# Second graph pass: the x strip on its own semaphore, the second mean square from the variance, the last two strips' keys stacked by SP

## What is computed

```python
def _L0_gnn_ref(x, adj, W):
    A_hat = adj + jnp.eye(adj.shape[0])
    d_inv_sqrt = jnp.sum(A_hat, axis=1) ** (-0.5)
    A_norm = d_inv_sqrt[:, None] * A_hat * d_inv_sqrt[None, :]
    return jax.nn.relu(A_norm @ (x @ W.T))

x = x + _L0_gnn_ref(_layernorm(x), adj, W)      # x1 in the kernel
z = _layernorm(x)                               # (x - mean) / sqrt(var + 1e-5)
h = z * rsqrt(mean(z * z) + 1e-6) * ln1_w       # the attention's input norm
q, k, v = h @ wq.T, h @ wk.T, h @ wv.T          # q and k are then rotated by cos, sin
...                                             # attention, experts
```

## Time and profile before

| | us |
|---|---|
| median of three runs | 3701.52 (3696.71 to 3705.01) |
| the profiled execution | 3697.04 |
| its span on the core | 3695.3 |

### The profile page before, as it was taken

The page is one execution under the profiler, slowest core; times in us unless marked ns, Lnnn a source line. Parts: engine busy times, 40 slices in busy tenths (PEclk is TensorE's granted clock), DMA queues, the critical chain, the costliest instruction groups (busy, mean ns, idle before and its releaser), DMA issues. The chain is left out here.

```text
span 3695.3 us, 56800 instructions
## 1 busy us (share of the span) xinstructions
PE 3115.2 (84%) x22369; PEld 1368.1 (37%) x22369; DVE 2580.5 (70%) x2752; ACT 1424.4 (39%) x2843; POOL 1690.7 (46%) x1094
## 2 busy tenths in 40 slices
PE   2578898999677884999999999999999999839990
PEld 1334443444333342343333333333333333315650
DVE  8888786773343443778878987877987898326773
ACT  0000000000000001565666666666666666735660
POOL 0000000002111111566788688877689778744653
PEclk9778999999888996999999999999999999969995
DMA  9898777676555762542221000000000000012226
GB/s 378 351 398 354 318 318 289 251 305 226 213 221 212 278 252 74 201 147 79 92 91 61 13 15 22 13 7 7 7 18 17 10 4 16 11 53 66 75 64 230
DMA packets 170238, 531.94 MB, mean 144 GB/s; under 512 B 20721, under 2 KB 66554, under 8 KB 125062
## 3 DMA queue, kind: packets, MB, share of 16 engines
q1 hardware_dynamic: 123752, 473.35, 33.3%
q10 hardware_dynamic: 33024, 31.47, 2.6%
q0 software_dynamic: 13200, 23.50, 2.0%
HBM read 434.70 MB, written 92.15 MB: 143 GB/s over the span
## 5 line engine op out<-in xcount | busy, mean ns | idle before, releaser
L1202 DVE TENSOR_REDUCE unit_max<-ps_max 128x2 f32<-128x1024 f32 (+2 forms) x1088 | 1226.1, 1171 | 310.5 <-PE ps_max L1431 265.6
L978 POOL TENSOR_TENSOR chunk_sum<-chunk_sum,probs 128x1024 f32<-128x1024 f32 x480 | 1132.2, 2359 | 307.9 <-ACT probs L1072 297.8
L1072 ACT ACTIVATE probs<-ps_ring 128x512 f32<-128x512 f32 x2112 | 1089.8, 595 | 437.1 <-PE ps_ring L1450 403.1
L537 PE MATMUL ps_gather<-ring,keep_attended 128*128 128x512 f32 x1688 | 803.1, 633 | 138.3 <-DMA ring<-in_adj 115.1
L1450 PE MATMUL ps_ring<-q_stack,keep_shared 97*128 97x512 f16 x2112 | 673.4, 385 | 27.8 <-ACT probs L1072 22.1
L1465 PE MATMUL ps_acc<-probs,keep_shared 128*32 128x256 f32 (+1 forms) x8448 | 565.6, 386 | 0.0
L537 PEld LDWEIGHTS ps_gather<-ring,keep_attended 128*128 128x128 f32 x1688 | 338.2, 205 | 548.4 <-issue 548.4
L352 DVE TENSOR_TENSOR work<-work,ring 128x2048 f32<-128x2048 f32 x195 | 446.7, 2291 | 38.8 <-DMA ring<-in_adj 35.0
L322 POOL DMA_DIRECT2D scratch_lower<-lower x13 | 7.3, 559 | 803.7 <-ACT lower L460 803.7
L1431 PE MATMUL ps_max<-k_heads,q_heads 32*128 32x512 f16 (+3 forms) x2176 | 277.0, 379 | 74.9 <-DVE unit_max L1202 48.2
L1474 PE MATMUL ps_acc<-probs,keep_ones_heads 128*32 128x256 f32 (+1 forms) x4224 | 326.9, 378 | 0.0
(11 more groups left out here) (239 smaller groups left out, 2742.3 us busy)
## 6 DMA issues: line engine op xcount, KB each, us to landing
ring<-in_adj SPq DMA_DIRECT2D x302, 1024.0 KB, 14.1
keep_shared<-in_adj SPq DMA_DIRECT2D x45, 1024.0 KB, 10.2
scratch_slots<-empty_rows SPq DMA_DIRECT2D x16, 2080.0 KB, 14.1
scratch_parts<-empty_part SPq DMA_DIRECT2D x8, 2048.0 KB, 13.3
moe_parts<-scratch_parts SPq DMA_DIRECT2D x64, 256.0 KB, 4.5
moe_x_rows<-scratch_slots SPq DMA_DIRECT2D x39, 260.0 KB, 2.7
x_in<-in_x SPq DMA_DIRECT2D x16, 256.0 KB, 13.2
x_in<-in_x ACTq DMA_DIRECT2D x16, 256.0 KB, 4.1
```

What stands on the lines that cost most here:

```text
L537: last = nc.tensor.matmul(bank[:], support[:, s * SUB + c, :], tile_of[g, is_again][:, c * BT:(c + 1) * BT], start=(first and c == 0), sto ...
L978: steps.then(nc.gpsimd.tensor_tensor(totals, totals, weights, ALU.add))
L1072: nc.scalar.activation(probs[:, q % SLOTS, i, kv, :, lo:], halves(bank)[:, :, lo:], ACT.Exp, scale=SCALE).then_inc(ring_read, 1)
L1202: nc.vector.tensor_reduce(unit_max[:, half % 2, heads, s % 2, unit], ps_max[:, base:base + HEADS, at:at + width], AX_X, ALU.max).then_inc( ...
```

## The change

- x has its own semaphore. Its load moves from behind `rotate(n)` to behind the first square root of `normalize(n)`, ahead of the stores of x1 and z. L411 waits for x alone. cos and sin stay where they were, under a new semaphore `tables_loaded`, for which `rotate` waits.
- The sum of squares of the centred rows is kept in `centered_sum`, and the mean square of z is taken from it as sum / C / std / std: three instructions on 128 x 4 values in the place of two on 128 x 512 and one on 128 x 4.
- The keys of the last two strips (n = 14 and 15) are stacked by SP, behind its last ring loads, under `last_stacked`. POOL issues those of the first fourteen and ends after its subtractions. SP waits for all stackings at the stage's end.

```diff
+        STACKED_BY_POOL = NB - 2
+        def stack_keys(queue, n, stacked):
+            cols = slice(finished[n] * BT, (finished[n] + 1) * BT)
+            for kv in range(NKV):
+                row = kv * NREP * HD
+                for part, src in ((0, k_hi), (1, k_lo), (2, k_hi)):
+                    queue.dma_start(keep["k_stack"][part * HD:(part + 1) * HD, kv, cols],
+                                    src[row:row + HD, :]).then_inc(stacked, 16)
...
                 for s in again[t]:
                     load_group((t, s), True)
+            for n in range(STACKED_BY_POOL, NB):
+                sp.wait_ge(stack_ready, 1)
+                sp.wait_ge(split_ready, 2 * n + 2)
+                stack_keys(sp, n, last_stacked)
+            sp.wait_ge(keys_stacked, 96 * STACKED_BY_POOL)
+            sp.wait_ge(last_stacked, 96 * (NB - STACKED_BY_POOL))
...
-                dve.wait_ge(strip_loaded, n * 48 + 48)
+                dve.wait_ge(strip_loaded, n * 16 + 16)
...
-                mean_square(nc, steps, z, squares[:], var[:], RMS_EPS).then_inc(var_ready, 1)
+                steps.then(nc.vector.scalar_tensor_tensor(out=var[:], in0=centered_sum[:], scalar=1.0 / C, in1=inv_std[:],
+                                                          op0=ALU.mult, op1=ALU.mult))
+                steps.then(nc.vector.tensor_tensor(var[:], var[:], inv_std[:], ALU.mult))
+                nc.vector.tensor_scalar(var[:], var[:], RMS_EPS, None, ALU.add).then_inc(var_ready, 1)
...
+                dve.wait_ge(tables_loaded, n * 32 + 32)
                 dve.wait_ge(qk_ready, n + 1)
...
                     if norm == 0:
+                        if n + 1 < NB:
+                            load_strip(n + 1)
                         act.wait_ge(z_ready, n + 1)
...
                 act.wait_ge(high_ready, n + 1)
                 if n + 1 < NB:
-                    load_strip(n + 1)
+                    load_tables(n + 1)
```

More of the change, by code:

```diff
@@ L173, in graph_stage @@
         std = sb("std", [P, SUB])
+        centered_sum = sb("centered_sum", [P, SUB])
         root_degree = sb("root_degree", [P, SUB])
@@ L208, in graph_stage @@
         strip_loaded = sem("strip_loaded")
+        tables_loaded = sem("tables_loaded")
         dve_step = sem("dve_step")
@@ L235, in graph_stage @@
         keys_stacked = sem("keys_stacked")
+        last_stacked = sem("last_stacked")
         block = ctx.enter_context(nc.Block())
@@ L332, in _ @@
                 pool.wait_ge(split_ready, 2 * n + 2)
-                cols = slice(t * BT, (t + 1) * BT)
-                for kv in range(NKV):
-                    row = kv * NREP * HD
-                    for part, src in ((0, k_hi), (1, k_lo), (2, k_hi)):
-                        pool.dma_start(keep["k_stack"][part * HD:(part + 1) * HD, kv, cols],
-                                      src[row:row + HD, :]).then_inc(keys_stacked, 16)
-            pool.wait_ge(keys_stacked, 96 * NB)
+                if n < STACKED_BY_POOL:
+                    stack_keys(pool, n, keys_stacked)
         @block.vector
@@ L414, in normalize @@
                 center(nc, steps, x1, centered[:], mean[:])
-                mean_square(nc, steps, centered[:], squares[:], var[:], LN_EPS).then_inc(var_ready, 1)
+                steps.then(nc.vector.tensor_tensor(squares[:], centered[:], centered[:], ALU.mult))
+                steps.then(nc.vector.tensor_reduce(centered_sum[:], squares[:], AX_X, ALU.add))
+                nc.vector.tensor_scalar(var[:], centered_sum[:], 1.0 / C, LN_EPS, ALU.mult, ALU.add).then_inc(var_ready, 1)
                 dve.wait_ge(std_ready, NB + n * 2 + 1)
@@ L428, in rotate @@
                     dve.wait_ge(split_stored, n * 48)
-                    dve.wait_ge(keys_stacked, n * 96)
+                    if n <= STACKED_BY_POOL:
+                        dve.wait_ge(keys_stacked, n * 96)
+                    else:
+                        dve.wait_ge(last_stacked, (n - STACKED_BY_POOL) * 96)
+                dve.wait_ge(tables_loaded, n * 32 + 32)
                 dve.wait_ge(qk_ready, n + 1)
@@ L476, in load_strip, with load_tables @@
             def load_strip(n):
+                act.dma_start(x_in[:], x_dram[finished[n]]).then_inc(strip_loaded, 16)
+            def load_tables(n):
                 t = finished[n]
-                act.dma_start(x_in[:], x_dram[t]).then_inc(strip_loaded, 16)
                 for tile, name in ((cos, "cos"), (sin, "sin")):
-                    act.dma_start(tile, dram[name][:, t * BT:(t + 1) * BT]).then_inc(strip_loaded, 16)
+                    act.dma_start(tile, dram[name][:, t * BT:(t + 1) * BT]).then_inc(tables_loaded, 16)
             act.wait_ge(x_read, NB)
             load_strip(0)
+            load_tables(0)
             for t in range(LAST - KEPT_SPAN, NB):
```

## The result

The changed kernel takes **3584.3 us** (median of four runs, 3581.3 to 3587.8) against 3699.1 (3696.7 to 3705.0) for the kernel before in the same comparison: a ratio of **0.9688, 95% interval 0.9670 to 0.9705**, some 115 us. The forecast was 3571, with a range of 3556 to 3607. The profiled execution took 3581.5 us, its span is 3579.8.

A forecast was written before the change was run, and what follows sets the result against it. Waits at L411 for loads in ACT's queue, holding up TensorE, were taken as the bound. 127.9 - 11 + 2.95 + 8.8 = 128.7 us off 3697.0 gave 3568.3, 3572.8 on the median's scale; forecast 3571, range 3556 to 3607.

The forecast's parts named there:

- What bounds the kernel: Second pass: no engine full; TensorE waits 108.4 us at L424, VectorE 111.4 at L411 for sin, one wait seen twice.
- The floor: Second pass, strip 0's turn to strip 15's, without waits: 15 x 22.31 + 12 x 3.43 = 375.8 us against 516.0.
- The residue in the second pass: Waits for stores late in ACT's queue after gathers, mainly strip 3: 11 us in all, ends 0 and 41.
- the margin: Nine strips that follow after five groups: with part 2 the chain takes 13.6 against a cover of 14.17, 0.6 to spare.
- the place sum of rows 7: ACT's queue beside a full ring: about 3.1 us a place, 4.6 places for x; leaves 0 to 2 in strips 6 and 8.
- The last strip: Uncovered chain behind the last turn: L411's 2.1 and part 2's 0.85 come off in full, 2.95 us.
- The stage's end: Barrier at line 146: POOL's drain becomes short, SP ends last at about 1435.9, 8.8 us gained.
- the bound for the long drain: Stage's end if POOL's drain stays long: barrier opens at 1431.1 + 9.0 = 1440.1, 4.6 us gained.
- Rival A: Stage's end: drain keeps its length or transfers' landing sets the end, so the queue change gives nothing: 3580; chance 0.12.
- B: The wait at L411 passes to the stores, five strips at 9.3 each, costing 46: 3617; chance 0.22.
- C: Slower: ACT's queue becomes the bound, the ring's queue never empty, 36 us of queue a strip: 3826; chance 0.03.
- D: No change: L411 finds x no earlier because another transfer holds the same place: 3697; chance 0.03.

The follow-up runs named there:

- the kernel with the early drain: Changed kernel with `lower` loaded behind the groups and x in 128 rows of 2 KB, plus a POOL drain behind strip 13's stacking: 3557.8 us, ratio 0.9640.

## Why the prediction was right, and where it was off

**What bounds the kernel** stood: the wait at L411 for what lay behind x in ACT's queue. The early load alone brings 99 of the 115 us, and the wait for sin is gone. The clock came back with it, 0.89 to 0.97.

**The floor** of 375.8 us stood too: the kernel in which POOL subtracts 32 columns comes to 381.1 us, 5.3 above it, with strip 0's 2.4 and the last gather (2.0) in it.

**The residue in the second pass** was the term that was mis-sized: 33.1 us above the floor instead of 23.3. By strips: strip 0 lost 2.2 (3.7 predicted; the slow group behind it did not come, and what is left falls together with POOL's L345), strip 4 lost 8.4 (6.8; the changed kernel's row names the ring load, where the earlier trace rows has only "issue"), strip 3 lost 11.1 (9.25), strips 6 and 8 lost 7.2 (1.75), the margin 2.0 in five strips (0), the rest 2.2 (1.8).
- Strip 3 was placed rightly, in the burst behind strip 0's gather, with nearly the right length, but by half of the mechanism. The step "cos and sin are issued where they were, with 17 us to the next `rotate` ...: nothing" looked at the tables and not at the third store that `rotate` waits for. k_hi, issued before x, landed after 18.3 us, and this delays strip 3 by 4.3 us before z delays it by another 4.5. z landed 45.4 us after the gather (SP goes on at 930.0), within the 44 to 46 of the forecast; as x's place was priced too high on the way, that closeness is in part luck.
- Strip 8's 6.2 is the same burst behind a later gather. "0 to 2" was the place sum of rows 7 carried on; x's place was too dear there (4.9 us for its rows instead of 11), and that of the ring's burst not measured at all.
- The margin of 0.6 was worked out with L411 at 0.69. That was its time behind a wait, when POOL was done. Without the wait it runs beside POOL's subtraction, at 1.53, 0.84 more, which turns 0.6 to spare into 0.3 short. The early load alone shows the same: 1.15 short of cover instead of 0.28. The forecast had named the sign for this ("TensorE waits about 1 us in all nine strips"); 0.3 came in six, 0.9 in one.

**The last strip** came off as said: 2.9 us for 2.95.

**The stage's end** gave 5.7 us for 8.8. The step that failed is "with the short drain the barrier opens there", for which the drain at the end of attention was taken as the nearer case. In that stage POOL issues 120 indirect transfers and not one direct one, so its 1.79 us could not tell what becomes of a drain behind 97 direct ones. The drain goes by the count of POOL's direct transfers in the stage, so two strips less shorten it by 12 x 82 ns = 1.0 us, and 4.6, the bound for the long drain, plus this 1.0 makes 5.6, which the measured 5.7 meets within the scatter of about 1 us. Rival A, that the drain keeps its length or the transfers' landing sets the end, is not what happens either: the kernel with the early drain shows that POOL's own transfers cost the time, at any moment that one asks for it.

**The rivals.** B, the wait passing to the stores, came true in two strips, for 17.3 us (4.3 of it at `rotate`, not at L411) where it had 46. C and D did not. (A's 8.6 should be the 8.8 of the sum; its 3580 stands.) The misses are 9.8 us in the second pass and 3.1 at the end, and the 128.7 us became 115.7, which makes the 13 us between the forecast and the result; the two untouched stretches differ by +4.0 and -3.7 and nearly cancel, which is luck.

## What to carry to other kernels

When a wait goes, re-time the instructions behind it: one that was measured after a wait can be slower where it now runs beside another engine. When a transfer is moved, list everything in the program that waits for any transfer of its queue, not only the moved one's reader. A wait of a loading engine that is followed by a burst of loads costs twice, at the load that comes late and at the other queues that the burst holds up; ordering the waiting load last took 18 us by the ratios here, 24 in the profiled second pass.

The fastest versions measured are the changed kernel with `lower` loaded behind the groups and what was put on top of it, at 3558 to 3561 us, 3.6 to 3.7% below the kernel before and, by the ratios, some 18 to 23 us below the changed kernel; among themselves their intervals overlap.

## What the runs showed of the hardware

- POOL's drain at the end of the graph stage took 82 to 83 ns for each direct transfer that POOL had issued since its last drain, however long ago it had landed: 4.56, 7.99, 8.97 and 9.05 us for 55, 97, 109 and 110. At the end of attention, behind 120 indirect transfers and no direct one, it took 1.79 us. ACT's, behind 128 transfers, took 8 ns, and SP's, behind more than 380, 7 to 124 ns.
- The same VectorE instruction with two inputs in SBUF took 0.69 us alone and 1.53 where it started during a subtraction on POOL. That subtraction took 1.60 us instead of 1.15 where it started during the VectorE instruction before.
- Beside a burst of eight 1 MB loads in SP's queue, a 128 KB store in ACT's queue, behind others, took 18.3 us to land and a 256 KB one 24.9; with the same loads issued one by one the longest landing of either was 14.0 us, and nothing waited for a store in strips 3 and 8.
